# State-space stage of a three-block kernel: step size as one fp32r product of three stacked parts, output bias as three bf16 parts, and another order of jobs

## The reference, cut to what matters

```python
xz = x @ in_proj_w + in_proj_b;  xc, z = split(xz)            # 2 x 512 channels
xc = silu(depthwise_conv4(xc) + conv_b)
delta_s, B, u = split(xc @ x_proj_w + x_proj_b, [16, 32])     # 16, 16 and 512 columns
delta = softplus(delta_s @ dt_proj_w + dt_proj_b)             # 512 channels
h = exp(-delta * n) * h + delta * B[n] * u                    # for n = 1..16, along the 512 tokens
y = (sum_n h + u * D) * silu(z)
x = x + y @ out_proj_w + out_proj_b
```

## Time and profile before

| what | value |
|---|---|
| time, median of 3 runs | 3438.0 us (3434.74 to 3440.54) |
| time of the profiled execution | 3436.78 us |
| its span, first to last instruction | 3434.7 us |
| state-space stage | from the start to about 1,770 us |
| busy over the whole span | PE 88%, DVE 71%, ACT 51%, POOL 65% |

### The profile page before, as it was taken

One profiled execution on the slowest core, in us unless ns is written; L12 is line 12 of the kernel. 1 busy time (PEld: TensorE's weight loads), 2 busy tenths in 40 slices (PEclk: granted clock), 3 DMA queues, 4 the chain that ended last, 5 costly groups with the idle time before them and its releaser, 6 DMA issues. The chain is left out here.

```text
span 3434.7 us, 54203 instructions
## 1 busy us (share of the span) xinstructions
PE 3009.1 (88%) x17168; PEld 2332.1 (68%) x17184; DVE 2425.9 (71%) x3701; ACT 1763.7 (51%) x3332; POOL 2235.8 (65%) x1403
## 2 busy tenths in 40 slices
PE   6899989999899998999857999896888876898988
PEld 2565655556555565556547889896767766898988
DVE  2888888888888888888855666664566654666674
ACT  3666666656666566665534444442333333444443
POOL 3878978888788887888855555562233335555554
PEclk9999999999999999999978999998999997999999
DMA  4321221112211122111144434342112214343442
GB/s 127 105 96 40 76 77 64 51 39 76 77 62 52 40 76 77 63 52 40 70 155 125 121 86 112 96 110 38 54 60 63 70 57 129 86 109 98 99 109 46
DMA packets 184203, 273.14 MB, mean 80 GB/s; under 512 B 35686, under 2 KB 156171, under 8 KB 175813
## 3 DMA queue, kind: packets, MB, share of 16 engines
q1 hardware_dynamic: 148676, 227.92, 20.5%
q0 software_dynamic: 35328, 42.76, 7.1%
HBM read 188.89 MB, written 94.72 MB: 83 GB/s over the span
## 5 line engine op out<-in xcount | busy, mean ns | idle before, releaser
L599 POOL TENSOR_TENSOR dbu<-du,bb 128x1024 f32<-128x1024 f32 x512 | 1199.1, 2360 | 153.5 <-DVE hs L738 148.7
L738 DVE TENSOR_TENSOR_SCAN hs<-da,dbu 128x1024 f32<-128x1024 f32 x512 | 1150.8, 2279 | 103.7 <-ACT da L686 36.3
L686 ACT ACTIVATE da<-delta 128x512 f32<-128x512 f32 x1024 | 570.2, 595 | 292.1 <-DVE hs L738 277.2
L838 PEld LDWEIGHTS yT<-ident,hs 128*128 128x128 f32 x4096 | 483.4, 146 | 168.0 <-issue 133.6
L838 PE MATMUL yT<-ident,hs 128*128 128x128 f32 x4096 | 540.6, 281 | 22.0 <-DVE hs L738 22.0
L1306 POOL TENSOR_TENSOR ffn_w_lo<-ffn_w,ffn_w_hi 128x512 fp32r<-128x512 f32 x256 | 373.8, 1479 | 132.1 <-ACT ffn_w_hi L1301 131.5
L1382 PE MATMUL ffn_ybank<-ffn_w_hi,ffn_hT_hi 128*128 128x256 f32 x1280 | 392.2, 306 | 74.2 <-DVE ffn_hT_lo L1370 74.2
L1383 PE MATMUL ffn_ybank<-ffn_w_lo,ffn_hT_hi 128*128 128x256 f32 x1280 | 378.0, 295 | 0.0
L1384 PE MATMUL ffn_ybank<-ffn_w_hi,ffn_hT_lo 128*128 128x256 f32 x1280 | 377.4, 295 | 0.0
L1352 PE MATMUL ffn_hbank<-ffn_rowsT_hi,ffn_w_hi 128*128 128x320 f32 x1024 | 321.8, 314 | 24.7 <-ACT ffn_h L1363 22.5
L1382 PEld LDWEIGHTS ffn_ybank<-ffn_w_hi,ffn_hT_hi 128*128 128x128 f32 x1280 | 260.9, 204 | 90.0 <-DVE ffn_hT_lo L1370 90.0
(11 more groups left out here) (233 smaller groups left out, 5243.3 us busy)
## 6 DMA issues: line engine op xcount, KB each, us to landing
bb<-b_rows SPq DMA_DIRECT2D x64, 1024.0 KB, 4.6
ffn_w<-L_ffn_W SPq DMA_DIRECT2D x64, 1024.0 KB, 10.1
slots<-empty SPq DMA_DIRECT2D x40, 530.0 KB, 6.7
ffn_rows<-slots SPq DMA_DIRECT2D x32, 662.5 KB, 5.1
xt<-L_attn_a_x SPq DMA_DIRECT2D x16, 512.0 KB, 3.9
x<-L_attn_a_x SPq DMA_DIRECT2D x16, 512.0 KB, 3.9
x_after_mamba<-x SPq DMA_DIRECT2D x16, 512.0 KB, 3.0
a_x<-x_after_mamba SPq DMA_DIRECT2D x16, 512.0 KB, 5.0
```

The source lines that it names most:

```text
L599: pool.tensor_tensor(dbu[:, s % DEEP], du[:, dt, :].unsqueeze(1).to_broadcast([P, SN, T]), bb[:, q * SN:(q + 1) * SN, :], ALU.mult).then_i ...
L686: ins = act.activation(da[:, s % 2, i, :], delta[:, par, dt, :], ACT.Exp, scale=-float(q * SN + i + 1))
L738: dve.tensor_tensor_scan(flat[0], flat[1], flat[2], 0.0, ALU.mult, ALU.add).then_inc(scanned.sem, 1)
L838: mm = pe.matmul(yT[:, j * P:(j + 1) * P], hs[:, s % DEEP, i, j * P:(j + 1) * P], k.ident[:], start=False, stop=(q == QS - 1 and i == SN - ...
```

## The change

Arithmetic. The 16 columns of `delta_s` stand three times in `w_x` (columns 0, 32 and 64 of 112; B moves to 96), so that the small product yields three copies. ACT writes rows 0 to 95 as fp32r into `db` and, in an instruction of its own, B into `b_turn`. DVE then writes over rows 32 to 63 with what the fp32r rounding lost (`delta_low`). The weights are split once: rows 0 to 63 rounded to fp32r, rows 64 to 95 what that lost. One fp32r product over 96 rows then gives high x high + low x high + high x low. The output bias stands as three bf16 parts in rows 0, 32 and 64, against three rows of ones. Both tables are made once, by DVE, from raw copies in the tile `x1`: the weights (two instructions) in turn 0 after step 12, the bias (six instructions) in turn 1 after step 0; the first load of `x1` waits for this. At the start there are 21 transfers of constants where there were 11, and POOL clears `x1` and some more pieces.

```diff
-XW = DI + 48
+XW = DI + 112
...
-RING_JOBS = ("G3", "Z0", "O0", "U2", "T0", "T1", "U3", "I0", "I1", "G0", "O1", "Z1", "I2", "I3", "RT0", "S", "DA0",
-             "DA1", "RT1", "DA2", "DA3", "G1", "RL", "U0", "Z2", "U1", "G2", "RP", "Z3", "-")
-MM_JOBS = ("G3", "Z0", "U2", "T0", "O0", "T1", "U3", "I0", "I1", "G0", "O1", "Z1", "I2", "I3", "RT0", "S", "DA0",
-           "DA1", "RT1", "DA2", "DA3", "G1", "RL", "U0", "Z2", "G2", "U1", "RP", "Z3")
-ACT_JOBS = ("U2", "T0", "T1", "U3", "RT0", "S", "DA0", "DA1", "RT1", "DA2", "DA3", "U0", "U1")
-DVE_JOBS = ("G3", "Z0", "O0", "I0", "I1", "G0", "O1", "Z1", "I2", "I3", "G1", "RL", "Z2", "G2", "RP", "Z3")
+RING_JOBS = ("G3", "Z0", "U2", "O0", "T0", "T1", "I0", "U3", "I1", "O1", "G0", "I2", "Z1", "I3", "S", "RT0", "DA0",
+             "DA1", "G1", "RT1", "DA2", "DA3", "RL", "Z2", "U0", "U1", "RP", "G2", "Z3", "-")
+MM_JOBS = ("G3", "Z0", "U2", "T0", "T1", "O0", "I0", "U3", "I1", "G0", "O1", "I2", "Z1", "I3", "RT0", "S", "DA0",
+           "DA1", "G1", "RT1", "DA2", "DA3", "RL", "Z2", "U0", "U1", "RP", "G2", "Z3")
+ACT_JOBS = ("U2", "T0", "T1", "U3", "RT0", "DA0", "DA1", "RT1", "DA2", "DA3", "U0", "U1")
+DVE_JOBS = ("G3", "Z0", "O0", "I0", "I1", "G0", "O1", "Z1", "I2", "I3", "S", "G1", "RL", "Z2", "G2", "RP", "Z3")
...
-        w_dt, w_out = sb("w_dt", [32, DI]), sb("w_out", [P, ND, C])
+        w_dt, w_out = sb("w_dt", [96, DI], F32R), sb("w_out", [P, ND, C])
...
-        b_db, w_conv, b_conv = sb("b_db", [48, 1]), sb("w_conv", [P, ND, DC]), sb("b_conv", [P, ND])
+        b_db, w_conv, b_conv = sb("b_db", [112, 1]), sb("w_conv", [P, ND, DC]), sb("b_conv", [P, ND])
...
-        b_out, one_row = sb("b_out", [32, C]), sb("one_row", [32, P])
+        b_out, one_row = sb("b_out", [96, C], BF16), sb("one_row", [96, P], BF16)
...
-        db = sb("db", [48, T])
+        db, b_turn = sb("db", [96, T], F32R), sb("b_turn", [112, T])
...
-        FIRST_CONSTS, CONSTS, ROUTE_CONSTS = 4, 11, 1 + 2 * E
+        FIRST_CONSTS, CONSTS, ROUTE_CONSTS = 4, 21, 1 + 2 * E
...
+            for i in range(3):
+                at = 32 * i
+                sp.dma_start(raw_dt[at:at + NS, :], w["dt_proj_w"]).then_inc(loaded, 16)
+                sp.dma_start(raw_dt[at + NS:at + NS + 1, :], w["dt_proj_b"].rearrange("(a n) -> a n", a=1)).then_inc(loaded, 16)
+                sp.dma_start(raw_b[at:at + 1, :], w["out_proj_b"].rearrange("(a n) -> a n", a=1)).then_inc(loaded, 16)
+            sp.wait_ge(bias_one, 4)
+            for i in range(3):
+                sp.dma_start(b_db[32 * i:32 * i + NS, :], w["x_proj_b"][0:NS].rearrange("(n a) -> n a", a=1)).then_inc(loaded, 16)
+            sp.dma_start(b_db[96:112, :], w["x_proj_b"][NS:2 * NS].rearrange("(n a) -> n a", a=1)).then_inc(loaded, 16)
...
         def load_x1(sp, row):
+            if is_turn(row, 0):
+                sp.wait_ge(staged, STAGED)
...
         def store_b(sp, turn, par):
-            wait_taken(sp, turn, "S")
-            sp.dma_start(k.b_rows[par], db[32:48, :]).then_inc(b_st.sem, 16)
+            sp.wait_ge(s_split.sem, s_split.at(turn, 2))
+            sp.sem_inc(sp_held, 1)
+            sp.dma_start(k.b_rows[par], b_turn[96:112, :]).then_inc(b_st.sem, 16)
...
-            act.activation(db[:], bank_of("S")[0:48, :], ACT.Identity, bias=b_db[:]).then_inc(act_took.sem, 1)
+            act.activation(db[0:96, :], bank_of("S")[0:96, :], ACT.Identity, bias=b_db[0:96, :]).then_inc(s_split.sem, 1)
+            act.activation(b_turn[96:112, :], bank_of("S")[96:112, :], ACT.Identity,
+                           bias=b_db[96:112, :]).then_inc(s_split.sem, 1)
...
+        def delta_low(dve, turn):
+
+            dve.wait_ge(s_split.sem, s_split.at(turn, 2))
+            dve.scalar_tensor_tensor(db[32:64, :], bank_of("S")[32:64, :], b_db[32:64, :], db[32:64, :].bitcast(F32),
+                                     ALU.add, ALU.subtract).then_inc(dve_took.sem, 1)
+
+        def stage_weights(dve):
+
+            dve.tensor_copy(w_dt[:], raw_dt).then_inc(staged, 1)
+            dve.wait_ge(staged, 1)
+            dve.tensor_tensor(w_dt[64:96, :], raw_dt[64:96, :], w_dt[64:96, :].bitcast(F32), ALU.subtract).then_inc(staged, 1)
+
+        def stage_bias(dve):
+
+            dve.tensor_copy(b_out[:], raw_b).then_inc(staged, 1)
+            dve.wait_ge(staged, 3)
+            dve.tensor_tensor(raw_b, raw_b, b_out[:], ALU.subtract).then_inc(staged, 1)
+            dve.wait_ge(staged, 4)
+            dve.tensor_copy(b_out[32:64, :], raw_b[32:64, :]).then_inc(staged, 1)
+            dve.tensor_copy(b_out[64:96, :], raw_b[64:96, :]).then_inc(staged, 1)
+            dve.wait_ge(staged, 6)
+            dve.tensor_tensor(raw_b[64:96, :], raw_b[64:96, :], b_out[64:96, :], ALU.subtract).then_inc(staged, 1)
+            dve.wait_ge(staged, 7)
+            dve.tensor_copy(b_out[64:96, :], raw_b[64:96, :]).then_inc(staged, 1)
...
-                mm = pe.matmul(bank[0:48, :], w_x[:, d, DI:], hx[:, d, :], start=(d == 0), stop=(d == ND - 1))
+                mm = pe.matmul(bank[0:112, :], w_x[:, d, DI:], hx[:, d, :], start=(d == 0), stop=(d == ND - 1))
...
-            pe.matmul(bank, w_dt[:, m * P:(m + 1) * P], db[0:32, :], start=True, stop=True).then_inc(ring_mm.sem, 1)
+            pe.matmul(bank, w_dt[:, m * P:(m + 1) * P], db[0:96, :], start=True, stop=True).then_inc(ring_mm.sem, 1)
```

More of the change, by code:

```diff
@@ L996, in one_turn @@
                             conv_input(act, turn, 0)
-                        if s == 9 and main:
+                        if s == 8 and main:
                             summed_copy(act, turn, row, 0)
-                        if s == 9 and first:
+                            skip_input(act, turn, row, 3)
+                        if s == 10 and first:
+                            tanh_x(act, turn, 0)
+                        if s == 12 and first:
                             conv_input(act, turn, 1)
-                        if s == 10 and main:
-                            skip_input(act, turn, row, 3)
@@ L1022, in one_turn @@
+                        if s == 20 and late:
                             route_turned(act, turn, 0)
-                        if s == 19 and is_turn(turn, 0):
+                        if s == 20 and is_turn(turn, 0):
                             act.wait_ge(loaded, 16 * CONSTS)
                             act.wait_ge(skip_ready, 1)
-                        if s == 20 and first:
+                        if s == 21 and first:
                             delta_b(act, turn)
-                        if s == 21 and first:
+                        if s == 22 and first:
@@ L1140, in one_turn @@
                             in_proj(pe, turn, 1 - par, "Z0", ND + 0)
-                        if s == 0 and late:
-                            out_proj(pe, turn, 0)
-                        if s == 0 and main:
                             x_proj(pe, turn, 2, 0)
                             x_proj(pe, turn, 2, 1)
-                        if s == 1 and first:
+                        if s == 0 and is_turn(turn, 2):
+                            pe.wait_ge(staged, STAGED)
+                        if s == 1 and late:
+                            out_proj(pe, turn, 0)
@@ L1147, in one_turn @@
+                        if s == 2 and first:
                             turn_x(pe, turn, 0)
-                        if s == 1 and late:
+                            turn_x(pe, turn, 1)
+                        if s == 2 and late:
                             out_proj(pe, turn, 1)
-                        if s == 2 and first:
-                            turn_x(pe, turn, 1)
-                        if s == 2 and main:
+                        if s == 3 and first:
+                            in_proj(pe, turn, par, "I0", 0)
@@ L1162, in one_turn @@
+                        if s == 8 and late:
+                            out_proj(pe, turn, 2)
+                        if s == 9 and main:
+                            turn_back(pe, turn, row, 0)
                         if s == 9 and first:
                             conv_taps(pe, turn, 1)
-                        if s == 10 and main:
-                            turn_back(pe, turn, row, 0)
-                        if s == 10 and late:
-                            out_proj(pe, turn, 2)
+                        if s == 9 and late:
@@ L1184, in one_turn @@
-                        if s == 15 and first:
+                        if s == 14 and is_turn(turn, 0):
+                            pe.wait_ge(loaded, 16 * CONSTS)
+                            pe.wait_ge(staged, 2)
+                        if s == 15 and first:
+                            x_proj_small(pe, turn, 0)
+                        if s == 15 and late:
+                            route_turn(pe, turn, turn - 2, 0)
+                        if s == 16 and first:
                             x_proj_small(pe, turn, 1)
-                        if s == 16 and first:
+                        if s == 18 and first:
@@ L1187, in one_turn @@
```

(28 more changed lines are left out.)

144 lines of the change are left out of this document (70 added, 74 removed).

## The result

The changed kernel takes **3506.6 us** (median of 4 runs, 3499.5 to 3510.8); the kernel before, run beside it, 3439.3 (4 runs, 3434.7 to 3440.6). Ratio 1.0196, 95% interval 1.0173 to 1.0219: 2% slower. The forecast was 3397, with 3431 as the upper end.

What follows compares the result with a forecast made beforehand. A turn was bounded by PE's first sixteen steps, a hand-over, DVE's steps 20 to 31 and a tail. 14 turns x 3.0 us, less 1, gave 41 off 3436.8; adding 1.2 gave 3397 us, range 3352 to 3431.

Steps and rivals of the forecast that it cites:

- POOL's sends and rstd move within its own order ... 0: POOL's jobs in a turn: moving the sends and rstd was claimed to cost 0.
- PE's stretch up to sum 16 becomes 62.4 - 1.3 - 1.85 = 59.3: PE's first sixteen steps: shorter by the bias saving (1.3 us) and the second S half moved out (1.85).
- the bias products' true saving: Four bias products a turn on PE: forecast saving 4 x 0.32 = 1.3 us, bounds 0 and 1.8.
- sum 16 at 62: Sign that the forecast is wrong: PE's sum 16 begins at 62, not 59 to 60, PE waiting for late inputs.
- the start: Turns 0 and 1: bias staging, `delta_low` and the B copy add 2 us; constant transfers and memsets add 0.
- From sum 16 to the end of scan 31: The turn's late part: sum 16 at 59.3 and scan 31 ending at 96.5, mostly at DVE's pace.
- The third `ysb` copy: ACT's copy that PE waits for: ends 5.2 us earlier, PE's wait shrinking from 3.85 to about 2 us.
- The S product: Four small products on PE: weight loads grow from 48 to 112 columns, taken as 0, at most 0.7 us a turn.
- The tail: End of the turn after scan 31: 5.5 us instead of 6.6, as Z3 now follows sum 31.
- Slower: Rival, chance 0.09: S waits for a late `silu_x` 3, 2.4 us a turn slower, 3472 us.
- The chain eats it: Rival, chance 0.14: `delta_low` and the second copy make the Ln 2 us later; 0.5 us a turn gained, 3430.
- the step-size saving: Step-size products on PE: 2.7 us a turn saved, counted as 0 because DVE sets the pace after sum 16.

Runs made afterwards that it cites:

- early2: The changed kernel with two POOL moves: softplus 0 back after step 27, sends after steps 1 to 8; 3428.5 us, ratio 0.9975.
- early_both: early2 with another turn 0, bias staging moved there, and two ACT jobs moved; 3414.7 us against 3449.8, ratio 0.9905.
- Runs 1, 2 and 5: The changed kernel with POOL waiting out the router's placement (3464.6 us); with sends after steps 2 to 9 again (3479.5 us); and early2 (3428.5 us).
- Run 10: early2 with two ACT jobs moved: uD3 behind decay 9, conv_input 1 behind decay 11; ratio 0.9945.
- Run 9: early2 with turn 0 reordered on PE and ACT, and the bias staging moved from turn 1 to turn 0; ratio 0.9935.
- arith2: The kernel before with the new arithmetic in the old order, step-size products after steps 18 and 20; 3462.1 us, ratio 1.0071.
- runs 6 and 7: The kernel before, old arithmetic, in the change's order (3563.6 us, 1.0378); the same with early2's POOL places (3503.2 us, 1.0186).

## Why the prediction was wrong

Direction, size and range were wrong; 0.08 was all that slower got. In the turns without the loop's branch, counted as in the forecast (other turns of a run differ by 0.1, in early_both by up to 0.7):

| mark, us | before | forecast | after | early2 | early_both |
|---|---|---|---|---|---|
| sum 16 begins | 62.4 | 59.3 | 66.8 | 61.7 | 60.6 |
| S complete | 62.4 | 62.6 | 70.0 | 64.9 | 63.7 |
| Ln and table load end | 79.7 | 79.2 | 86.7 | 81.6 | 80.6 |
| third `ysb` copy begins | 85.5 | 80.3 | 87.8 | 82.6 | 81.6 |
| scan 31 ends | 98.45 | 96.5 | 104.0 | 98.7 | 97.7 |
| turn | 105.0 | 102.0 | 110.3 | 105.1 | 104.0 |

**The step that failed first** is "POOL's sends and rstd move within its own order ... 0". It was costed for POOL and its scans alone. What failed is that POOL runs without a gap where DVE places tokens: 5.6 us of DVE a turn, ahead of scan 0, which nothing hides. Runs 1, 2 and 5 change only POOL and get 42, 25 and 68 us of turns 2 to 15 back; in early2 a turn without the branch is 5.2 us shorter than in the changed kernel.

**The second** is "PE's stretch up to sum 16 becomes 62.4 - 1.3 - 1.85 = 59.3. No other job enters or leaves this stretch". No job did, but they met late results: early2 has sum 16 at 61.7, with four waits on PE, 3.4 us in all, where before there was none (its PE timeline, from 611.45):

```profile
622.64 1.09 PE L821 MATMUL ring<-ident,xt 128*128 128x128 f32 x8 [0.45 <-DVE sz L731]
...
642.98 0.28 PE L891 MATMUL ring<-b_out,one_row 96*128 96x256 bf16 x1 [1.08 <-DVE hx L726]
...
647.60 2.84 PE L836 MATMUL ring<-xc,w_diag 128*128 128x512 f32 x6 [1.30 <-ACT last_tap L633]
...
665.80 2.84 PE L836 MATMUL ring<-xc,w_diag 128*128 128x512 f32 x6 [0.57 <-ACT last_tap L633]
```

With them, and with the bias products' true saving, the forecast's own sum comes out: 62.4 - 2.0 - 1.85 + 3.4 = 61.95. So even with POOL mended an ordinary turn saves nothing, 105.1 for 105.0, where the forecast had 3.0. I had argued that later jobs cost nothing where PE didn't wait, and never placed ACT's `conv_input` 1, moved from step 9 to 12, against PE's convolution. Run 10 moves two ACT jobs and gets 0.9 us a turn back. I had named sum 16 at 62 as what would prove the forecast wrong, by PE waiting for "ysb1 or conv_input 3, now 3 steps later", and gave it no price; the job that moved three steps is `conv_input` 1, and the longest of the four waits is for it.

**The third** is the start: +12.7 instead of +2, from the order of turn 0 and the staging. Run 9 takes both away together and gets 12.6 back, by its rows 7.2 from the order (the Ln) and the rest from the staging. The Ln stays 4.0 us later than before; in arith2, with the old order, it is 0.6 later, so little of that is the arithmetic or its transfers. **Turn 16** was to lose nothing and took 101.0 instead of 93.0; with POOL mended 96.2. What the remaining 3 us are I didn't look into.

**What held.** From sum 16 to the end of scan 31 the forecast had 37.2 us; measured are 37.2 after, 37.0 in early2, 37.1 in early_both. `delta_low` waits 0.32 us for the B copy. The third `ysb` copy costs PE 2.07 us in early2 instead of 3.85. The S product's loads grew from 122 to 177 ns and its four products still take 1.88 us: 0, as taken. The rule of the Trainium skill ("TensorE: Matmul & The Clock Gate", LDWEIGHTS), an estimated 53 ns for 64 more columns, agrees with the growth (55 ns), but nothing of it was exposed. The bias product gained all that it could: it stands 0.11 us ahead of the next product instead of 0.62, 2.0 us a turn instead of 1.3. The bound of 1.8 was mis-summed: with the 0.19 gone too it is 4 x (0.62 - 0.11) = 2.0. From 200 to 1600 us of the changed kernel:

```profile
L891 PE MATMUL ring<-b_out,one_row 96*128 96x256 bf16 x51 | 14.0, 274 | 0.0
```

Two step-size products take 0.57 us instead of 1.91, a saving of 2.9. The tail was 6.3 instead of 5.5: Z3 behind sum 31 saved 0.3, not 1.1.

**The rivals.** "Slower" had the sign, and 3472 was the nearest number, but not the mechanism: S is late because scan 0 and with it sum 16 is. "The chain eats it" (3430) is close to what early2 does (3428.5), by way of PE's waits rather than of the chain. And the step-size saving, "worth 0 there", is not worth 0: of 4.9 us that the arithmetic takes from PE (2.0 and 2.9), 3.9 to 4.4 come through by runs 6 and 7, more than the bias products have. In this order U is what PE has late for DVE, after the step-size products as well; no run took the two savings apart.

## What to carry to other kernels

When a change moves a job on one of VectorE or GpSimd, lay the two timelines over each other: short VectorE instructions with SBUF inputs must stand where GpSimd is idle, or be put in a form that isn't held (a reduction, a PSUM input), and a group mean that is ten times the neighbours' mean in the view of lines is the sign. In an order written by hand, give every moved job the time at which its input arrives from the other engine before calling it free; and read the first turn by itself, where nothing hides a chain. A forecast from one turn holds for that turn: here the mended order saves 0 in the turn that was read and 3.7 us in those at the loop's branch.

## What the runs showed of the hardware that I had not expected

- A DVE instruction on 4 or 8 numbers a partition takes up to one whole POOL instruction (2.4 us) beside back-to-back POOL work. POOL isn't slowed: `dbu` has a mean of 2363 ns after and 2360 before.
- It isn't only two-input operations: a plain copy (1.44 us), a `tensor_scalar` (0.84 mean, 1.80 longest) and casts (1.50, 2.32) are held as well; the reductions (L349, L364), the reciprocal (L351) and the instruction with a PSUM input (L805) are not.
- A row of such instructions pays again each time: 1.4, 2.4 and 2.3 us one after the other, each ending with a POOL instruction.
